# Two attentions overlapped on one core: the first attention's end cut into single instructions spread over the second attention's steps, the next row's projections moved ahead of it, and its input loaded twice

## The reference

```python
x = layernorm(x + differential_attention(x))  # 16 heads of size 8, two softmaxes: a = a1 - lam*a2
                                              # RMS norm per head, times norm_w, then @ wo
x = layernorm(x + fp4_ffn(x))                 # gate/up/down, inputs and weights rounded to FP4 in blocks of 16
x = layernorm(x + causal_gqa_attention(x))    # 16 query heads, 4 KV heads, size 64, rotary
x = layernorm(x + moe_top1(x))                # 8 experts, 128 -> 512 -> 128
```

## Time and profile before

| | us |
|---|---|
| median of 3 runs | 1482.98 (1474.93 to 1483.29) |
| profiled execution | 1472.26 |
| its span | 1470.5 |
| PE busy | 1177.6 (80%) |
| DVE busy | 800.8 (54%) |
| ACT busy | 648.2 (44%) |
| POOL busy | 466.3 (32%) |

### The profile page before, as it was taken

The page is one execution under the profiler, slowest core; times in us unless marked ns, Lnnn a source line. Parts: engine busy times, 40 slices in busy tenths (PEclk is TensorE's granted clock), DMA queues, the critical chain, the costliest instruction groups (busy, mean ns, idle before and its releaser), DMA issues. The chain is left out here.

```text
span 1470.5 us, 18597 instructions
## 1 busy us (share of the span) xinstructions
PE 1177.6 (80%) x6601; PEld 566.5 (39%) x6601; DVE 800.8 (54%) x1852; ACT 648.2 (44%) x1456; POOL 466.3 (32%) x495
## 2 busy tenths in 40 slices
PE   2788545888978769899878769899978688989686
PEld 1112121222444424344445424344445455455454
DVE  4677327683865476563865376663875322666212
ACT  1267312675355226665355226666255223255122
POOL 2000024000869040000869040000779030399000
PEclk6579655788999769999989769999989789999799
DMA  5600030000002000000002000000000000000000
GB/s 147 155 2 2 8 86 0 2 1 2 1 8 75 12 1 2 2 2 8 1 8 72 15 1 1 2 2 8 1 1 1 1 0 1 8 1 1 1 0 8
DMA packets 28811, 23.88 MB, mean 16 GB/s; under 512 B 12264, under 2 KB 25648, under 8 KB 27952
## 3 DMA queue, kind: packets, MB, share of 16 engines
q1 hardware_dynamic: 28720, 22.70, 5.9%
HBM read 14.96 MB, written 7.34 MB: 15 GB/s over the span
## 5 line engine op out<-in xcount | busy, mean ns | idle before, releaser
L701 DVE TENSOR_REDUCE mx<-ps 128x1 f32<-128x512 f32 x512 | 324.0, 683 | 179.6 <-PE ps L1149 177.8
L927 ACT ACTIVATE PROB<-ps 128x512 f32<-128x512 f32 x512 | 274.2, 602 | 203.2 <-PE ps L1140 202.4
L428 POOL TENSOR_SCALAR PROB<-PROB,rsum 128x128 f32<-128x128 f32 (+3 forms) x256 | 277.7, 1102 | 43.6 <-DVE rsum L803 43.2
L969 ACT ACTIVATE PROB<-ps,mx 128x128 f32<-128x128 f32 (+3 forms) x256 | 132.9, 524 | 190.4 <-DVE mx L798 187.3
L1149 PE MATMUL ps<-kst,qst 24*128 24x512 bf16 x512 | 157.3, 455 | 49.5 <-DVE mx L701 26.4
L891 ACT ACTIVATE MREG<-ps,b_sb 128x512 f32<-128x512 f32 x128 | 88.1, 689 | 180.6 <-PE ps L1077 180.0
L1171 PE MATMUL ps<-PROB,v 128*32 128x512 f32 x1024 | 162.0, 713 | 3.7 <-ACT OREG L936 2.4
L798 DVE TENSOR_REDUCE mx<-ps 128x1 f32<-128x128 f32 (+3 forms) x256 | 113.1, 484 | 93.7 <-PE ps L1215 93.4
L1229 PE MATMUL ps<-cst,PROB 128*128 128x128 f32 x640 | 111.2, 296 | 59.6 <-POOL PROB L428 23.4
L1077 PE MATMUL ps<-xnT,w_sb 128*128 128x512 f32 x256 | 148.7, 683 | 10.1 <-DVE MREG L646 5.6
L1140 PE MATMUL ps<-qst,kst 27*128 27x512 bf16 x512 | 131.0, 418 | 27.1 <-ACT PROB L927 15.2
(11 more groups left out here) (178 smaller groups left out, 1302.9 us busy)
## 6 DMA issues: line engine op xcount, KB each, us to landing
qk_terms<-RREG SPq DMA_DIRECT2D x48, 128.0 KB, 2.1
kst<-qk_terms SPq DMA_DIRECT2D x16, 192.0 KB
qst<-qk_terms SPq DMA_DIRECT2D x16, 192.0 KB
w_sb<-in_L_ffn_W_dram SPq DMA_DIRECT2D x1, 2048.0 KB
qst<-mrow SPq DMA_DIRECT2D x96, 4.0 KB
XN<-in_L_attn_x_dram SPq DMA_DIRECT2D x4, 256.0 KB, 2.9
out_dram<-XP SPq DMA_DIRECT2D x4, 256.0 KB, 2.3
wq_sb<-in_L_attn_Wq_dram SPq DMA_DIRECT2D x1, 512.0 KB, 4.9
```

Of the source, the lines that this page charges most:

```text
L428: pool.tensor_scalar(tile, tile, rsum1[:, 2 * v + half:2 * v + half + 1], None, ALU.mult).then_inc(scaled1, 1)
L701: dve.tensor_reduce(mx0[:, ga % 2, col:col + 1], ps[:, max_banks[MAX_SLOT[n] % len(max_banks)], :], AX, ALU.max, negate=True).then_inc(slo ...
L927: act.activation(prob0[:, s % 2, q % 4, q % 8 // 4], ps[:, s0_banks[q % len(s0_banks)], :], ACT.Exp, scale=float(HD0) ** -0.5).then_inc(ex ...
L969: act.activation(prob1[:, half, at:at + w], ps[:, a1_bank(v, half), 0:w], ACT.Exp, bias=mx1[:, col:col + 1], accum_out=sum1[:, col:col + 1 ...
```

## The change

The end of the first attention is dealt out over steps 5 to 35, one or two DVE instructions a step, each with its wait on the one before at the start of the next step instead of right behind it. POOL's rounding is one pass a step in 28 to 31. The next row's input goes into the free buffer `ZC` as soon as SP comes to it, and the projections take steps 6 to 16; the row is loaded a second time into `XN` (`fetch_again`), after the terms, for the residual sum. PE's output projection of the first attention moves to step 19, the transposes to step 35.

```diff
             def fetch(k):
+                if k:
+                    sp.wait_ge(xn_turned, k)
+                sp.dma_start(ZC[:, :, :], x_rows[k]).then_inc(x_in, 16)
+
+            def fetch_again(k):
                 if k:
                     sp.wait_ge(att0_sum, k)
-                    sp.wait_ge(proj0, 3 * k)
-                sp.dma_start(XN[:, :, :], x_rows[k]).then_inc(x_in, 16)
+                sp.dma_start(XN[:, :, :], x_rows[k]).then_inc(xr_in, 16)
...
             store_parts(0)
             load_terms(0)
+            fetch_again(0)
             for dst, src in loads:
                 sp.dma_start(dst, src, allow_slow_non_contiguous=True).then_inc(weights_in, 16)
...
                     fetch(r + 2)
                     store_parts(r + 2)
                     load_terms(r + 2)
+                    fetch_again(r + 2)
...  POOL: quantise yields after each of its four passes, settle() at the start of the next
-                if k < BATCH and v == 20:
-                    pool.wait_ge(xs_ready, k + 1)
-                    for _ in quantise(XQ[:, :], ZB[:, :, :].rearrange("p t n -> p (t n)"), T, xq_ready):
-                        pass
-                if nx < BATCH and v in (22, 25):
-                    split_next(nx, (v - 22) // 3)
+                if k < BATCH and 28 <= v < 32:
+                    if v == 28:
+                        pool.wait_ge(xs_ready, k + 1)
+                    next(rounds)
+                if nx < BATCH and v in (11, 14):
+                    split_next(nx, (v - 11) // 3)
...  DVE (each v holds the same instructions as before, settle() first)
+            def outputs0(k, v):   # v 5 reciprocal, 6 times lam, 7 and 8 products, 9 difference,
...                                # 11 square, 12 sum, 14 reciprocal, 15 product, 17 and 18 times norm_w
+            def input0(k, v):
+                if v == 20:
+                    dve.wait_ge(y0_ready, k + 1)
+                    dve.wait_ge(xr_in, 16 * (k + 1))
+                    dve.tensor_tensor(ZB[:, :, :], XN[:, :, :], tiles(7), ALU.add).then_inc(att0_sum, 1)
...                                # 21 statistics, 23 reciprocal and two tiles of XA, 24 the other two,
...                                # 25 block maxima, 26 scales, 27 division and exponent
-                    if v in (20, 23):
-                        rest_of_next(nx, (v - 20) // 3)
-                    if v == 26:
+                    if v in (10, 13):
+                        rest_of_next(nx, (v - 10) // 3)
+                    if v == 16:
                         values_of_next(nx)
...  DVE in overlap, before the experts' sum is written to ZC
                     dve.wait_ge(y1_ready, i + 1)
+                    dve.wait_ge(xn_turned, min(i + 3, BATCH))
...  ACT
-                    if v == 9:      (square root of the RMS norm)
+                    if v == 13:
-                    if v == 15:     (square root of the layernorm)
+                    if v == 22:
-                    if v == 17:     (turn_next; high_of_next 19, 22 -> 9, 12; copy_xT 30 -> 35)
+                    if v == 7:
...  PE
             def turn_next(k, bank=7):
                 pe.wait_ge(x_in, 16 * (k + 1))
                 if k:
-                    pe.wait_ge(att0_sum, k)
+                    pe.wait_ge(o0_kept, NG * k)
                 for t in range(NT):
-                    ins = pe.transpose(ps[:, bank, P * t:P * (t + 1)], XN[:, t, :], ident)
+                    ins = pe.transpose(ps[:, bank, P * t:P * (t + 1)], ZC[:, t, :], ident)
...
-                    if k < BATCH and v == 12:
+                    if k < BATCH and v == 19:
                         pe.wait_ge(on_ready, NT * (k + 1))
+                        if nx < BATCH:
+                            pe.wait_ge(v0_ready, nx + 1)
...  turn_next 16 -> 6, project_next 18, 21 -> 8, 11, project_v_next 24 -> 14
-                    if k < BATCH and v == 28:
+                    if k < BATCH and v == 35:
                         pe.wait_ge(xq_ready, k + 1)
...
+                        pe.wait_ge(att0_sum, k + 1)
                         transpose_tiles(xq, 7, x_turned)
```

More of the change, by code:

```diff
@@ L719, in _ @@
             o_u = oall[:, :].rearrange("p (a u x d) -> p u a x d", a=4, u=2, d=HD0 + 1)
-            def outputs0(k, part):
-                if part == 0:
-                    dve.wait_ge(o0_kept, NG * (k + 1))
[L725 to L730, removed]
-                    settle()
[L732 to L735, removed]
+            blocks = lambda t: t.rearrange("p (b q) -> p b q", q=QB)
@@ new lines, in block_max, with block_scale @@
+            def block_max(src, n):
+                step(dve.tensor_reduce(q_sc[:, 0, 0:n // QB], blocks(src), AX, ALU.max, apply_absolute_value=True))
+            def block_scale(n):
+                s, r = q_sc[:, 0, 0:n // QB], q_sc[:, 1, 0:n // QB]
+                settle()
+                step(dve.tensor_scalar(s, s, 1.0 / 6.0, 1e-12, ALU.mult, ALU.max)); settle()
+                step(dve.reciprocal(r, s)); settle()
+                step(dve.tensor_scalar(r, r, 1.0 - 2.0 ** -24, None, ALU.mult))
@@ L749, in sum0 @@
[L749 to L758, removed]
-                rows = lambda t: t.rearrange("p t n -> p (t n)")
-                scales(rows(XA[:, :, :]), XQ[:, :], rows(ZB[:, :, :]), T, step, settle, xs_ready)
@@ L762, in turn @@
[L762 to L777 removed]
+                if v == 14:
+                    dve.wait_ge(rms_ready, k + 1)
+                    step(dve.reciprocal(rms[:, 0], rms[:, 1]))
@@ new lines, in outputs0 @@
+                if v == 15:
+                    settle()
+                    w = rms[:, 0].rearrange("p (g a) -> p g a", a=1).broadcast_to([P, 4 * 4 * NT, HD0])
+                    step(dve.tensor_tensor(o0, o0, w, ALU.mult))
+                if v in (17, 18):
+                    settle()
+                    o4 = od[:, 0].rearrange("p a (q j) d -> p q a j d", q=NT)
+                    for q in (2 * (v - 17), 2 * (v - 17) + 1):
+                        dst = on[:, :, :, q].rearrange("p d (j a) -> p a j d", a=4)
+                        dve.tensor_tensor(dst, o4[:, q], nw_sb[:, :].rearrange("p (j a d) -> p a j d", a=4, d=HD0), ALU.mult).then_inc(on_ready, 1)
@@ new lines, in input0 @@
+            def input0(k, v):
[3 more added lines that the diff above has]
+                    dve.tensor_tensor(ZB[:, :, :], XN[:, :, :], tiles(7), ALU.add).then_inc(att0_sum, 1)
+                if v == 21:
+                    dve.wait_ge(att0_sum, k + 1)
+                    centre(ZB, bnB, mvB, varB)
+                if v == 23:
+                    dve.wait_ge(stdB, 2 * k + 1)
+                    step(dve.reciprocal(stB[:, 1], stB[:, 0])); settle()
+                if v in (23, 24):
+                    for t in (2 * (v - 23), 2 * (v - 23) + 1):
+                        ins = dve.tensor_scalar(XA[:, t], ZB[:, t], mvB[:, t, 0:1], stB[:, 1, t:t + 1], ALU.subtract, ALU.mult)
+                        if t < NT - 1:
+                            step(ins)
+                        else:
+                            ins.then_inc(lnB, 1)
+                rows = lambda t: t.rearrange("p t n -> p (t n)")
+                if v == 25:
+                    dve.wait_ge(lnB, 2 * k + 1)
+                    if k:
+                        dve.wait_ge(hq_ready, k)
+                    settle()
+                    block_max(rows(XA[:, :, :]), T)
+                if v == 26:
+                    block_scale(T)
+                if v == 27:
+                    over_scale(rows(XA[:, :, :]), XQ[:, :], rows(ZB[:, :, :]), T, xs_ready)
```

76 lines of the change are left out of this document (46 added, 30 removed).

## The result

| | before | after |
|---|---|---|
| median, us | 1482.42 | 1438.26 (4 runs, 1436.92 to 1440.72) |
| ratio to before, 95% interval | | 0.9719 [0.9689, 0.9749] |
| profiled execution | 1472.26 | 1440.72 |
| its span | 1470.5 | 1438.9 |

The change makes the kernel 2.8% faster, where 1.6% were forecast (1459 us). The two profiled executions are 31.5 us apart, the medians 44: the profiled execution of before was faster than the four timed ones beside it.

What follows compares the result with a forecast made beforehand. POOL and PE together were taken to bound the attention stages, a chain of latencies stage -1. Terms -10.3, -14.1 and +0.5 gave -23.9 us on 1472.26, ratio 0.9838, applied to the median 1482.98: 1459 us; range 1436 to 1477.

Steps and rivals of the forecast that it cites:

- full cover: Rival: the dealt-out pieces vanish entirely and only POOL's own work is left; 1430 to 1450 us, chance 0.20.
- Stage -1: In `attention1(-1)`, early projections bring the terms before the second `GATE_UP` ends, removing PE's 10.29 us stall: -10.3, bounds -9 and -12.
- Attention stages: `attention1(0)` to (2): excess over undisturbed `attention1(3)` (105.0 if warm) falls from 18.9, 21.2 and 15.7 us; together -14.1.
- DVE, 2.4 charged: Per attention stage: pieces in steps without a gap cost 1.4 us, those in steps 5 and 21 0.5 each.
- 1.0 for waiting against POOL: Per attention stage: DVE instructions take longer beside a busy POOL; +1.0 us, bounds 0 and 4.
- ACT, 2.5 charged: Per attention stage: square roots with two table loads each delay step 13 by 2.2 us and step 22 by 0.3.
- Rounding, 4.5 charged: Per attention stage: POOL's four passes take 5.5 us, the fourth behind the last scaling, so they cost 4.5.
- Next row, 3.0 charged: First two attention stages: PE's projections beside POOL's splitting, steps 6 to 14, 4.0 us less 1.0 hidden behind ACT's wait.
- The clock: Second attention stage: some 2.3 of its 21.2 us excess is lower clock, half given back; that stage -5.5.
- Setup: The second load of row 0 delays SP ahead of the weights: +0.5 us, up to +1.9.
- the third: Rival: DVE's pieces wait for POOL, or the clock falls while POOL rounds; only stage -1 saves, 1468 to 1478, chance 0.21.
- The fourth: Rival, slower: PE, POOL, DVE and ACT in one loop, each piece delays the next step; 1497 at 85% paid, chance 0.06.

Runs made afterwards that it cites:

- the dealing experiment without early projections: Changed kernel, but the row loaded once, into `XN`, after the residual sum, and the next row's projections in steps 22 to 32; 1455.19 us, ratio 0.9814.
- the second profile: The kernel before the change, unedited, profiled once more; 1478.7 us, span 1476.9.
- the bursts: Changed kernel with DVE's end of the first attention back in steps 8, 12, 18, 21 and 27, POOL's four passes all in step 28; 1464.18 us.
- Two edits that took 1.8 and 2.0 us off the third stage: Changed kernel with both ACT.Sqrt as ACT.Exp, 1436.22 us; rounding on DVE and row 0 loaded once, plus ACT's first square root in step 14: 1437.42 us.

## Why the prediction was right, and where its sizes were off

The mechanism was right on both counts, the size in one. 24 us were forecast and 44 measured. The time of 1438 lies only 2 us inside the lower end of the stated range, 1436, which was set to take in most of the case of full cover; that it lies inside is in part luck. *Stage -1*: the terms are hidden behind the second `GATE_UP`, -11.0 measured for -10.3, and the dealing experiment without early projections takes it back (46.8). `xT` is next, as written, and POOL's passes stand in its chain: moving them gave 3.2.

*Attention stages*: -24.1 measured, -14.1 forecast. The step that was mis-sized is the cost left after dealing out: 11.5 and 14.5 us over the undisturbed stage were forecast, 9.5 and 11.1 remain (114.50 and 116.06 less 105.0). By term:

- DVE, 2.4 charged, and 1.0 for waiting against POOL: nearly nothing where tested. Taking 2.8 us of DVE out of a stage gave 0.06, 0.07 and 0.4. The scaling into `XA` takes 462 ns, below the 561 of the earlier trace rows, though POOL rests less. By the Trainium skill's SBUF — State Buffer, Who interferes with whom, an instruction of DVE with two SBUF inputs and one of GpSimd that reads SBUF exclude each other. The rival that every piece would wait half a scaling, 8 us a stage, is not borne out: in `attention1(0)` of the changed kernel the difference (L769) takes 676 ns and the scaling by blocks (L752) 675, against 691 and 694 in stage -1, where POOL mostly rests. Five groups are longer (the products L766, for example, 876 ns against 692), by 1.9 us together.
- ACT, 2.5 charged: 1.8 in the third stage; in the other two POOL took the first square root's part of it, and the rest can't be told from the clock.
- Rounding, 4.5 charged: 2.8 when it is taken off POOL in the third stage, 0.8 of it PE's busy time at a higher clock; DVE's passes may hold a part of what they replace.
- Next row, 3.0 charged: 1.6 (116.06 less 114.50).
- The clock: half of the second stage's loss was forecast to come back; all of it came back (0.93 to 0.96). The third stage stands at 0.93 in the earlier trace rows as well and came back to 0.96, and the forecast had no term for that. In `attention1(3)`, with nothing edited, a rise from 0.95 to 0.98 was worth 2.5 us; by that, an estimate, some 2.5 us of the third stage's 6.2 are the clock's, and without them its forecast of 4.2 was not too low.

In the third stage these overcharges come to 5.4 us, but of the 9.5 that remain only 5.0 (2.8, 1.8 and 0.4) are pinned by an experiment; 1.1 is PE's output projection, not tested, and 3.4 have no term. That leaves the forecast 2.0 us off there, 3.4 in the first stage and 4.6 in the second. The terms were tested one at a time and partly at another clock, so their sum is a rough one.

*Setup*: +0.5 forecast, up to +1.9; the first row of maxima is 2.1 us later, since SP's issues behind the load take longer too. The other 2.4 us up to the first reciprocal are open: the clock in `overlap(-1)` falls differently in nearly every kernel, and the reciprocal comes between 167.6 and 173.4 us. The three kernels that come below 168 all load row 0 only once, but so do those with 170.2 and 170.7.

*The base*: the ratio was formed on one execution, 10 us below the median of the timed ones. On the profiles it is 1440.72 / 1472.26 = 0.979, where 0.984 was forecast; the medians give 0.972. The other 0.7% is the spread of the kernel before; of its 10 us the second profile, 6.4 us longer than the first, found 4.9 in `overlap(1)` and 1.7 in `attention1(0)`, at a lower clock.

The rivals: full cover (1430 to 1450) is the case that the time of 1438 fell into by its number, not by its mechanism: it would have left 5.5, 5.5 and 2.0 us over the undisturbed stage, and 11.1, 11.1 and 9.5 remain. Part of what keeps the stages from that bound is POOL's rounding and ACT. Of the third, the fall of the clock behind POOL's passes is there in small: from 456 to 464 us the granted clock is 0.55, and the last product with the values takes 3.76 us instead of 2.37, but L1297's successor takes 7.41 as before. The fourth, the loop paying for every piece, is not what happens even with the bursts: they pay 57.9 of its 94 us, 61%, where it needed 70% to be slower than before.

## What to carry to other kernels

Where engines hand work round a loop in a fixed order, look at the longest piece of side work between two of the loop's own instructions, not only at its sum. In this kernel 12 us of DVE's work a stage, in five bursts instead of single instructions, cost about 20 us more over three stages, half of it in matmuls at a lower clock, and cutting 2.8 us out of the single ones gave nothing. Put independent work with a long DMA behind it first, and pay with a second load if a buffer stands in the way. Work that stays on the saturated engine was not hidden by dealing it out; moving the rounding to DVE, which is not part of the change, gave 17 us more; of the 16.3 us between the two profiles 11.4 lie in the stages that it touches and the rest where nothing was edited.

## What the runs showed of the hardware that was not expected

The granted clock is worth as much here as a good edit, and an edit far from it moves it. Four 64x512 score matmuls took 1.13 us at the higher level and 2.08 at the lower. Both times the fall came after PE had waited longer than usual for POOL. Two edits that took 1.8 and 2.0 us off the third stage made the other two 1.7 to 3.1 us longer, and with one of them unedited stretches got over 10 us longer. Why the clock falls where it does is open. A difference of under 10 us between two versions of this kernel says something about the schedule only when it is seen, stage by stage, at the same clock.
